# Rows through DRAM for three quarters of the tokens in the first expert layer of a three-layer mixture-of-experts kernel

## What is computed

```python
h = scan(lambda prev, xt: tanh(xt @ Wx + b + prev @ Wh))        # 32 steps, 64 batches at a time
x = x + h + shared(h) + sum_e g[e] * (gelu(h @ We1[e]) @ We2[e])  # 31 experts, 128 -> 128 -> 128
```

## Time and profile before

| | |
|---|---|
| median of 3 runs | 495.77 us (494.96 to 496.07) |
| profiled execution: time, span | 490.89 us, 489.1 us |
| mean granted PE clock | 0.939 of full |
| busy us PE, DVE, ACT, POOL | 434.6, 401.1, 354.3, 199.2 |
| moved by DMA | 76.38 MB, 156 GB/s |

### The profile page before, as it was taken

The page is one execution under the profiler, slowest core; times in us unless marked ns, Lnnn a source line. Parts: engine busy times, 40 slices in busy tenths (PEclk is TensorE's granted clock), DMA queues, the critical chain, the costliest instruction groups (busy, mean ns, idle before and its releaser), DMA issues.

```text
span 489.1 us, 8870 instructions
## 1 busy us (share of the span) xinstructions
PE 434.6 (89%) x2354; PEld 362.4 (74%) x2354; DVE 401.1 (82%) x937; ACT 354.3 (72%) x771; POOL 199.2 (41%) x192
## 2 busy tenths in 40 slices
PE   8998999999999999899988999999945999888840
PEld 7984687777877777688676888888824999888740
DVE  2578499999999999999898699988975887777622
ACT  2344588888898888899888878788723998877630
POOL 2226144444244444333001000623570488788870
PEclk9996699999999999999998999999966999999975
DMA  4892345555944444446399421200018674566516
GB/s 106 206 256 80 121 165 176 181 183 190 316 172 172 172 172 172 172 178 230 136 351 363 135 64 46 89 17 30 31 57 228 190 137 108 149 149 173 116 29 229
DMA packets 49589, 76.38 MB, mean 156 GB/s; under 512 B 9173, under 2 KB 36630, under 8 KB 45718
## 3 DMA queue, kind: packets, MB, share of 16 engines
q1 hardware_dynamic: 38742, 60.43, 38.0%
q0 software_dynamic: 7648, 4.36, 6.2%
q10 hardware_dynamic: 3168, 11.22, 5.9%
HBM read 50.23 MB, written 18.77 MB: 141 GB/s over the span
## 4 chain that ended last, share of the span: by engine, by line
PE 42%; DVE 27%; issue 13%; DMA 8%; ACT 3%; POOL 2%; SPq 1%; ACTq 1%; DVEq 1%; POOLq 0%
PE ps L1391 9%; DVE hid_lo L1087 9%; PE ps L1392 8%; PE ps L1393 8%; PE ps L1676 6%; DVE hid_lo L1176 4%; DVE yg L1081 4%; DMA out_dram<-xtok 4%; PE ps L1678 2%; DMA gb<-gt_d 2%; PE ps L1461 2%; PE ps L1456 1%; DVE c_f L1196 1%; PE ps L1417 1%; DVE yg L1188 1%
## 5 line engine op out<-in xcount | busy, mean ns | idle before, releaser
L1087 DVE TENSOR_TENSOR hid_lo<-yg,hid_hi 128x512 fp32r<-128x512 f32 x124 | 97.5, 786 | 0.0
L812 ACT ACTIVATE hid<-ps,bias_cur 128x512 f32<-128x512 f32 x128 | 86.5, 677 | 11.4 <-PE ps L1393 10.4
L833 ACT ACTIVATE hid_hi<-yg 128x512 fp32r<-128x512 f32 x124 | 77.9, 628 | 20.4 <-DVE yg L1081 19.5
L647 POOL TENSOR_TENSOR w2l<-raw,w2h 128x128 fp32r<-128x128 f32 x32 | 25.4, 792 | 108.0 <-ACT w2h L782 108.0
L716 POOL DMA_INDIRECT disp<-stage,idx x32 | 33.6, 1050 | 74.8 <-issue 54.7
L868 ACT ACTIVATE hid<-ps,cols 128x512 f32<-128x512 f32 (+3 forms) x84 | 52.8, 629 | 15.2 <-PE ps L1393 12.5
L1391 PE MATMUL ps<-in_hi,w1h 128*128 128x512 f32 x128 | 53.8, 420 | 6.3 <-POOL w1l L647 5.8
L1176 DVE TENSOR_TENSOR hid_lo<-hid,hid_hi 128x512 fp32r<-128x512 f32 (+3 forms) x84 | 48.5, 599 | 7.1 <-ACT hid_hi L872 6.0
L1081 DVE TENSOR_TENSOR yg<-hid,h_f 128x512 f32<-128x512 f32 x60 | 50.5, 841 | 1.4 <-DMA h_f<-gt_d 0.9
L1081 DVE TENSOR_TENSOR yg<-hid,gb 128x512 f32<-128x512 f32 x64 | 46.6, 728 | 6.0 <-ACT hid L812 5.8
L1392 PE MATMUL ps<-in_lo,w1h 128*128 128x512 f32 x128 | 51.4, 401 | 0.0
(11 more groups left out here) (242 smaller groups left out, 1189.4 us busy)
## 6 DMA issues: line engine op xcount, KB each, us to landing
gb<-gt_d SPq DMA_DIRECT2D x15, 1024.0 KB, 4.7
h_f<-gt_d SPq DMA_DIRECT2D x14, 1024.0 KB, 4.7
disp<-empty ACTq DMA_DIRECT2D x16, 616.5 KB, 6.6
w1d<-wf SPq DMA_DIRECT2D x15, 512.0 KB
rawf<-in_L_ffn_w_dram SPq DMA_DIRECT2D x16, 256.0 KB, 2.7
xrow_a<-disp SPq DMA_DIRECT2D x16, 137.0 KB, 3.3
raw<-in_L_ffn_We_dram SPq DMA_DIRECT2D x2, 960.0 KB, 8.4
nat<-in_x_dram SPq DMA_DIRECT2D x8, 128.0 KB, 3.2
```

Source lines behind the costliest of these rows:

```text
L812: nc.scalar.activation(hid0[:, m % 4, :], bank(4 + m % 4), ACT.Gelu, bias=bias0_cur[:, e_par:e_par + 1]).then_inc(s_hid0, 1)
L833: nc.scalar.activation(hid_hi0[:, m % 8, :], src[:, m % 4, :], ACT.Copy).then_inc(s_hi0, 1)
L1087: V.tensor_tensor(hid_lo0[:, m % 8, :], src[:, m % 4, :], hid_hi0[:, m % 8, :].bitcast(F32), ALU.subtract).then_inc(s_lo0, 1)
```

## The change

The last quarter (q = 3) and the shared expert stay dense: 4 items for the shared expert and 31 for the experts on quarter 3, 35 items. 19 of them run ahead of the rows, 16 behind. The other three quarters (T0 = 12 groups of 128 tokens) go by rows:

1. In the RNN PE turns h to rows (`rows_turn`), and counts each token's rank in its experts (`ranks0`); DVE makes its three slots (`places0`). Every expert has a region of 1536 + 256 rows in DRAM buffer xd. POOL scatters the token rows there, 12 indirect DMAs for a quarter (`scatter0`), 36 in all. SP writes 256 zero rows behind each expert's last row.
2. 48 tiles of 256 rows: one for each of the 31 experts, and 17 dynamic ones for what is beyond 256 rows (DVE finds them in `tables0`). Per tile: SP loads it, PE turns it (`turn0`), ACT and DVE split it, three matmuls of 256 columns (`first0`), ACT gelu twice (full and high half), DVE low half, six matmuls of 128 columns with the hidden rows as the stationary operand (`out0`), DVE copy, SP stores to yd. For dynamic tiles POOL copies the weights of the first product (w1d0), two tiles ahead.
3. POOL gathers three result rows for each token, 36 indirect DMAs, DVE weights and adds them (`combine`), PE turns them back (`back`), and they join the sum in x1. Quarter 0 is combined in the second dense part, quarters 1 and 2 beside items 3 to 8 of the second layer, whose order of quarters becomes 0, 3, 1, 2.
4. All weights of the first layer are split once into w1, w2 (blocks of four experts, [128 x 512]): high halves by ACT, from RNN step 16 on, low halves by DVE (blocks 0 to 3) and POOL (4 to 7). Splits of the second layer's weights move to POOL alone; those of wc2 stand between the dynamic tiles' copies. Means, gates and stores of the second layer move to later items, the third layer's weight splits from units 2 to 11 to units 6 to 15.

```diff
+SQ = 3
+T0 = 4 * SQ
+TR = 256
+DYN0 = (N_TOK0 * K0 - K0) // TR
+NT0 = E0 + DYN0
+DENSE = [(0, q) for q in range(J0)] + [(e, SQ) for e in range(1, N0)]
+NA = 15
+N_A = J0 + NA
+LAG0 = 3
...
@@ sync
+            sp.wait_ge(s_z0, J0)
+            sp.wait_ge(s_fill, 16 * (E0 + 1))
+            sp.wait_ge(s_disp, 16 * T0 * K0)
+            for t in range(XR0):
+                load0(t)
...
+            for t in range(NT0):
+                store0(t)
+                if t + XR0 < NT0:
+                    sp.wait_ge(s_tr, t + 1)
+                    load0(t + XR0)
...
+                if t == 24:
+                    sp.wait_ge(s_g3, SQ)
+                    for e in range(NC_):
+                        sp.dma_start(rawc2[:, e, 1, :].rearrange("p (c f) -> p c f", f=P),
...
@@ gpsimd
+            in_low(0)
+            scatter0(0)
+            in_low(1)
+            in_low(2)
+            scatter0(1)
+            in_low(3)
+            scatter0(2)
+            for b in range(VB, N_BLK):
...
+            pool.wait_ge(s_wc2, 16 * NC_)
+            pool.wait_ge(s_tab, 3)
+            expert_of0 = multi(tab0[0:1, 1, :], mybir.EngineType.Pool, E0)
+            for j in range(DYN0):
...
+                if j >= 2:
+                    pool.wait_ge(s_m1, t - 1)
+                    pool.wait_ge(s_thi, t - 1)
+                G.tensor_copy(w1d0[:, j % 2, :, :], w1[:, :, bass.ds(expert_of0[j], 1), :].rearrange(
...
+                if j % 2 and j // 2 < NC_:
+                    split_c(wc2, rawc2, j // 2)
+            for k in range(4):
+                pool.wait_ge(s_yst[k], 16 * (NT0 // 4))
...
@@ scalar
+            slots = (16, 18, 19, 20, 22, 23, 24, 26, 27, 28, 30)
...
@@ vector
+            for t in range(NT0 + 2):
+                if t < NT0:
+                    dve.wait_ge(s_thi, t + 1)
...
+                    V.tensor_tensor(hr_lo[:, t % 3, :], hr[:, t % 3, :], hr_hi[:, t % 3, :].bitcast(F32),
+                                    ALU.subtract).then_inc(s_tlo, 1)
+                if t >= 2:
+                    y_out(t - 2)
+                if t + 2 < NT0:
+                    x_low(t + 2)
+                if t == 18:
+                    results0()
+                if t in (20, 21, 22):
+                    gates3(t - 20)
+            items0(N_A, N_ITEMS0)
...
+                    if n in (3, 4):
+                        combine(1, n - 3)
...
+                    if n == 8:
+                        combine(2, 0)
+                        combine(2, 1)
+                    if n == 11:
+                        x1(3)
+                        x1_lo(3)
+                        for k in range(4):
+                            means(k)
...
@@ tensor
+            for t in range(NT0 + 2):
+                if t < NT0:
+                    first0(t)
+                if t + 2 < NT0:
+                    turn0(t + 2)
+                if t >= 2:
+                    out0(t - 2)
```

950 lines of the change are left out of this document (631 added, 319 removed).

## The result

The changed kernel takes 542.63 us (median of 4 runs, 540.08 to 546.09) against 495.37 of the kernel before (493.91 to 496.07): ratio 1.0963 [1.0889, 1.1036]. The forecast, 475.8 us and faster, was wrong in size and in sign. Its execution in the profile took 546.09 us, with a span of 544.4; the sum of the prediction stands for a span of 469. So 75 us have to be found.

What follows compares the result with a forecast made beforehand. It took dense items as PE-bound at 1.36 us. Item 22 of the second layer moves from 274.9 to 255, 20 us less: 490.9 becomes 471, plus 4.9 for the median, 475.8 us; range 458 to 495.

Steps and rivals of the forecast that it cites:

- The front: Stretch before the first gated item: last in_low ends at 57.4 us, last scatter at 73.4; item 3 began at 45.24 before.
- the RNN may grow: RNN: 3 us of ACT waiting for weights plus 2 for PE's transposes and rank matmuls, priced at nothing under POOL's chain.
- The cover: POOL's chain of in_low and scatters beside the RNN, 1.33 us a scatter, said to be 12 us longer than the RNN.
- The same cover hides DVE's table of tiles: Front: DVE's table of tiles, about 8 us, and two weight splits were said to lie hidden under POOL's chain.
- Items 3 to 18 then take 16 x 1.36: First dense part: 21.8 us, plus 3 for a half-clock start and DVE's weight splits, ending at 82.
- rival 2: Gathers cost 1.90 us each, like accumulating scatters or held up by DVE: 20.5 us more, 496, no change; chance 0.12.
- Row tiles: The 48 row tiles: 1.31 us each, 2.2 for ten while POOL splits wc2, running from 84 to 175 us.
- Rival 3: Row tiles: PE falls to half clock, 2.5 us a tile, 34 us more, 510 us; chance 0.07.
- The stand at tile 31: Row tiles: PE stands 5.5 us for POOL's first w1d copy, which waits for all wc2 raws, at 137.5 us.
- three signs of being wrong: Row stage begins before 75, PE does not wait for POOL at tile 31, or clock shows 0.5 between 90 and 130.
- Rows back and the join: 36 gathers at 1.33 us come last, landing at 228; then 27 us to item 22 of the second layer, at 255.
- The rest: From item 22 of the second layer to the end: the same work as before, so no change was priced.

Runs made afterwards that it cites:

- e3: Changed kernel with POOL waiting for DVE's table of tiles before its eight weight subtractions, a wait already met, so in effect the same code: 521.05 us.
- e1: Changed kernel with PE turning the gates of quarters 0 and 1 two or three RNN steps later, so it does not wait for DVE: 516.74 us.
- e11: Changed kernel with ACT making two weight casts in the RNN, at steps 29 and 30, instead of eleven from step 16 on: 526.13 us.
- first series: The runs e1, e2, e3 and e4, each a separate edit of the changed kernel, one execution each: 512.34 to 521.05 us.
- e2: Changed kernel with all 36 POOL scatters put behind the fourth in_low, so none runs beside the RNN: 517.46 us.
- e9: Changed kernel with e1's and e4's edits, earlier register load, later POOL wait for wc2 raws, and weight low halves, x_f sums, slot arithmetic on DVE: 500.87 us.
- e14: e9 with 5 gated dense items ahead of rows, not 15, DVE's extra work spread over tiles, wc2 loads and splits later: 491.41 us, lower runs' ratio 0.989.
- e4: Changed kernel with DVE's result slots and gates moved to tiles 4 to 8, and wc2 raw loads from tile 24 to tile 11: 512.34 us.
- e8: e2's edit of the changed kernel run again, all scatters behind the fourth in_low: 516.10 us.
- e15: e14 with all scatters behind the fourth in_low, so none runs beside the RNN: 503.77 us, ratio 1.0254.

## Why the prediction was wrong, by its own steps

**The front: "the RNN may grow ... priced at nothing, +5 at most if uncovered".** This failed. The cover itself was right: POOL's chain has the size forecast (e3: last in_low ends at 57.1 against 57.4, a scatter 1.28 against 1.33), and e1 got only 4 of its 11 us. But the RNN grew by 32 us, not 5, and came out on top of its cover. Of the 32, 11 are the clock, which PE's waits for DVE's gates brought down, and the waits themselves (e1 against e11, 14.8 us and 26.0), and 17 are late signals, which are in all three profiles of the unedited code and in none of the first series (42.8 against 26.0, cause open). 3 are the slow first steps, of which no run shows the cause. The casts, transposes and ranks, for which 2 us were counted, are 1 (e1's 14.8 against 13.8 before). The 3 counted for ACT's wait for the weights are right where the first steps are quick (e3: 2.68, to 24.5), and missing after the change, where they are slow. The prediction counted the instructions that the change puts on PE and ACT in the RNN, and not what it puts on DVE ahead of the gates, for which PE waits in order. Item 3 came 17.7 late.

**"The same cover hides DVE's table of tiles".** This failed. With the RNN's end at 67.7 there is no cover left, and the table's 8.5 us lie behind item 3, in the stretch that the next step prices.

**"Items 3 to 18 then take 16 x 1.36".** This failed by 32 us: 59 from item 3 to the first row tile, where 26.6 were forecast. The rate of the earlier trace rows was taken from a stretch where POOL hardly runs (2 of 10 us busy from 226 to 236, before). Of the 32, 13 are POOL's two-input work (e2 against e3), 9 of them the one DVE instruction locked out by its row of subtractions; each of its x_f sums holds DVE 1.1 us. 8.5 are the table. 3.5 are idle time of PE in front of the first row tile, where it loads the experts' numbers into registers. About 7 are left, in which the clock is low (0.67 from 68 to 100); these were not told apart, and the parts are differences between single profiles. e9 took 18 of the 32 back. The rule for this was in the text, as rival 2, with the Trainium skill's page "SBUF — State Buffer", but it was priced at the gathers only. There it costs little: a gather takes 1.40 with its gap beside 1.33 forecast. The place where it decides was the dense part, with POOL's two-input subtractions. The trace of before did show it, and I had not read that row (timelines of DVE, then POOL, before the change):

```profile
145.98 1.78 DVE L1087 TENSOR_TENSOR hid_lo<-yg,hid_hi 128x512 fp32r<-128x512 f32 x1
```

```profile
145.70 1.52 POOL L690 TENSOR_TENSOR wc<-rawc,wc  x1 [0.18 <-POOL wc L688]
```

One POOL subtraction of [128 x 512] turned 0.68 into 1.78. The changed kernel has eight of them in a row, plus four sums, in 16 items.

**Row tiles.** 1.31 was right at full clock (1.37; 1.57 in many tiles of e14, where DVE has one instruction more in each) and 2.5 at half was right too (2.35). The stage took 97 us against 91. Rival 3, priced at 34 more and given 0.07, came true in part: the clock was at 0.71 from 135 to 200. The stand at tile 31 was 7.8 against 5.5 and sat where it was said (shown by e4). Of the three signs of being wrong that the prediction named, one came: the clock shows 0.50 from 90 to 99, ahead of the rows.

**Rows back and the join.** Gathers as forecast but for 2 us, last to come as forecast. From the last gather's landing to item 22 it was 40 us against 27. This stretch was built from full-clock rates, and the clock there is low at first. From 264 to 300, after the change:

```profile
264.00:300.00 36.00, 21.13 (x68) 15.80 (x68) 16.89 (x40) 15.22 (x24) 16.18 (x17) 0.68 0.58 204
```

A late signal stands in the stretch as well:

```profile
ACT hid L1055 <- remote: 8.0, 1, 8.0
```

But e14 has 43 us there (280 - 235, less the 2.3) without late signals, at a clock of 0.96 to 250 and 0.89 behind it, with PE busy for 32 of 45 us. So neither explains the loss alone, and it stays in the best version. It was not taken apart.

**The rest, "priced at nothing"**: item 22 to the end is 218.6 us after the change against 214.3 before (489.1 - 274.85). The bound of nothing was 4 off.

**The sum.** +50 in front, +6 in the row tiles, +2 in the gathers, +13 in the join, +4 behind: 75. Without late signals the same code (e3, one execution) is 50 over the forecast, and still 5.8% slower than before (e2, e4 and e8, one execution each, 4 to 5%); so the sign does not hang on the unexplained part. e14, whose lower runs are 1.1% faster than before but whose median is equal to it, is free of the lock, and its mean clock is 0.895 against 0.833; the end of its profiled execution is still 24 above the forecast. No version tried was clearly faster than the kernel before in all its runs.

## What to carry to other kernels

Work saved is not time saved when it opens pauses: a pause of PE can be paid twice, once itself and once in matmuls at half clock behind it, so cost a new stage at both clocks and ask which engine's in-order wait stands in front of it. Before moving elementwise work to POOL, look in the trace for one DVE instruction beside one POOL instruction with two SBUF inputs, and count how many such rows would meet; give them to DVE or part them. When a change moves the last chain, an order that was free before has to be costed again (e2 and e15), and work counted as hidden has to be looked for again (the table of tiles). Before an edit is given the difference between two profiles, compare them ahead of the place that it touches: the first steps of e1 and e3 differ by 3.4 us.
